# Two groups of heads share one PSUM bank in the weighing of an attention and mixture-of-experts block

## The reference

```python
# attention: 16 heads of 8; q and k are normalised 6-component line products
q = lines(bg @ W1_q.T, bg @ W2_q.T)        # bg = [x, x of the token before]
k = lines(x @ W1_k.T, x @ W2_k.T)
logits = einsum('bhtc,bhsc->bhts', q, k @ J6.T) * 6**-0.5
attn = softmax(where(causal, logits, -inf))
o = einsum('bhts,bhsd->bhtd', attn, (x @ Wv.T + bv) by heads)
x = layernorm(x + o @ Wo.T + bo)
# experts: a shared one, and the best 2 of 8 weighted by sigmoid(x @ Wr.T + rb)
x = layernorm(x + shared(x) + sum_of_two(weight * expert(x)))   # silu(x Wg) * (x Wu) Wd
```

## Time and profile before

| | us |
|---|---|
| median of 3 runs (lowest, highest) | 990.3 (988.67, 993.97) |
| span of the profiled execution, first to last instruction | 846.3 |
| between that span and the median of the runs | 144.0 |
| TensorE busy in the span | 713.0 |
| VectorE | 652.2 |
| GpSimd | 605.9 |
| ScalarE | 585.3 |

### The profile page before, as it was taken

How to read it: one execution, slowest core, us unless ns; L and a number is a source line. 1 busy time by engine, 2 the same in 40 slices (tenths; PEclk the granted TensorE clock), 3 DMA queues, 4 the chain that set the end, 5 groups by cost and what they waited for, 6 DMA issues and landing times.

```text
span 846.3 us, 23791 instructions
## 1 busy us (share of the span) xinstructions
PE 713.0 (84%) x7568; PEld 455.1 (54%) x7568; DVE 652.2 (77%) x1712; ACT 585.3 (69%) x907; POOL 605.9 (72%) x901
## 2 busy tenths in 40 slices
PE   2689998899998998899999988886899999999700
PEld 2334554454544554445545543475788888887600
DVE  7647798988789889788798794689667666665795
ACT  1478897688786886687887887553466666665456
POOL 4436666689887987698898887653177777777585
PEclk8689999899999999899999998899999999999955
DMA  7000111111111111101201102622663333331496
GB/s 255 14 14 13 38 39 38 52 56 47 51 59 41 50 56 36 58 28 53 68 31 50 45 32 85 210 89 77 170 189 96 100 109 103 102 98 53 121 277 200
DMA packets 88797, 69.89 MB, mean 83 GB/s; under 512 B 8292, under 2 KB 77158, under 8 KB 88720
## 3 DMA queue, kind: packets, MB, share of 16 engines
q1 hardware_dynamic: 69456, 43.43, 17.8%
q0 software_dynamic: 8512, 17.06, 6.1%
q10 hardware_dynamic: 10752, 8.39, 3.3%
HBM read 38.16 MB, written 31.21 MB: 82 GB/s over the span
## 4 chain that ended last, share of the span: by engine, by line
PE 54%; DVE 25%; issue 9%; ACT 6%; POOL 5%; DMA 1%; DVEq 0%; ACTq 0%; POOLq 0%
PE S L905 14%; PE O L727 12%; PE O L927 8%; PE S L712 7%; PE W L686 4%; ACT probs L1071 3%; PE W L752 3%; POOL probs L540 2%; DVE prodA L1276 2%; PE W L662 2%; PE W L943 2%; POOL prodB L528 1%; DVE stats L1686 1%; DVE hid L1634 1%; DVE hid L1613 1%
## 5 line engine op out<-in xcount | busy, mean ns | idle before, releaser
L1071 ACT ACTIVATE probs<-S 128x1024 f32<-128x1024 f32 x320 | 322.7, 1044 | 95.5 <-PE S L712 70.3
L540 POOL TENSOR_SCALAR_AFFINE_SELECT probs<-probs 128x256 f32<-128x256 f32 (+1 forms) x448 | 228.8, 541 | 101.1 <-ACT probs L1071 100.5
L619 POOL DMA_INDIRECT z_scratch<-y,rows x136 | 139.2, 1023 | 63.5 <-issue 36.9
L727 PE MATMUL O<-probs,v_aug 128*32 128x512 f32 (+3 forms) x2048 | 172.9, 458 | 11.9 <-POOL probs L540 11.9
L263 POOL DMA_INDIRECT rows_scratch<-xrow,slot_i x128 | 131.7, 1029 | 44.6 <-issue 27.8
L712 PE MATMUL S<-qkT 32*128 32x512 f16 (+3 forms) x1024 | 137.6, 311 | 17.6 <-ACT probs L1071 9.7
L1634 DVE TENSOR_TENSOR hid<-hid 128x512 f16<-128x512 f32 x100 | 69.3, 693 | 72.4 <-ACT hid L1203 72.4
L1184 ACT ACTIVATE silu<-S 128x512 f32<-128x512 f32 x100 | 59.7, 597 | 91.3 <-PE S L905 90.7
L905 PE MATMUL S<-xT_rt,w_T 128*128 128x256 f16 (+1 forms) x864 | 103.5, 267 | 2.3 <-DVE xT_rt L1595 1.7
L927 PE MATMUL O<-w_T,hid 128*128 (+1 forms) x1200 | 91.5, 221 | 15.1 <-DVE hid L1634 11.7
L712 PEld LDWEIGHTS S<-qkT 32*128 32x128 f16 x1024 | 39.1, 92 | 112.1 <-issue 40.6
(11 more groups left out here) (158 smaller groups left out, 1131.7 us busy)
## 6 DMA issues: line engine op xcount, KB each, us to landing
rows<-rows_scratch SPq DMA_DIRECT2D x64, 130.0 KB
z<-z_scratch SPq DMA_DIRECT2D x32, 256.0 KB, 4.1
xT<-in_x_cols ACTq DMA_DIRECT2D x16, 256.0 KB, 2.8
x_in<-in_L_attn_x ACTq DMA_DIRECT2D x16, 256.0 KB, 3.1
x_scratch<-x SPq DMA_DIRECT2D x16, 256.0 KB, 2.6
x1T_scratch<-x1T SPq DMA_DIRECT2D x16, 256.0 KB, 2.2
xT_sh<-x1T_scratch SPq DMA_DIRECT2D x16, 256.0 KB, 4.4
x_in<-x_scratch SPq DMA_DIRECT2D x16, 256.0 KB, 5.0
```

Of the source, the lines that this page charges most:

```text
L540: pool.affine_select(out=v, in_=v, compare_op=ALU.is_ge, fill=0.0, base=0, pattern=[[0, v.shape[1]], [1, P]], channel_multiplier=-1).then_ ...
L619: pool.indirect_dma_start(out=z_dram, in_=y[:, q, a, :], in_offset=None, out_offset=bass.IndirectOffsetOnAxis(ap=rows[:, q, a, P + 1:P + 2 ...
L727: mm = pe.matmul(O[g % 2][32 * j:32 * j + 32, kb * P:T], v_aug[:, par, kb, 4 * g + j, :], probs[:, g % 2, c, col:col + T - kb * P], start= ...
L1071: act.activation(probs[:, g % 2, c, :], S[(g + c) % 2][:, :], ACT.Exp, scale=-SCALE / SPLIT_UP ** 2).then_inc(s_exp, 1)
```

## The change

Groups 0 and 1 now write the same output bank `O[0]`, groups 2 and 3 `O[1]`. In `v_aug` the heads j of groups 2p and 2p+1 lie in one slot of 82 columns. The weight tile for an even group has values and ones in columns 0 to 8 as before; that for an odd group has them in columns 9 to 17, with zeros on both sides. The odd group accumulates onto the even one: only its first product starts the bank, only the last one of the odd group ends it. So a strip of 32 partitions holds two heads, in 18 rows.

`copy_out` runs once for each pair, for groups 0 and 1 where group 1 was copied, for 2 and 3 where group 3 was. `transpose_out` runs in two halves, with two token blocks each: four transposes into `W1` after `logits(1, 0)`, four into `W0` after `logits(1, 1)`. `normalise` has a reciprocal of 128x32 and a product of 128x256 for each half. Counts of the semaphores follow. The columns of Wv and bv, and the rows of Wo, are permuted on the host to the new order of heads. Not shown below: the same replacement of counts in `transpose_o`, `down_early`, the last batch's part, and the count of VectorE's steps.

```diff
+PAIRS = 2
+SLOT = DH + 1
+VW = 32 + SLOT
...
         xres = sb("xres", [P, 2, NT, P])
-        oT_raw = sb("oT_raw", [P, HP, T])
+        oT_raw = sb("oT_raw", [P, PAIRS, T])
         rden = sb("rden", [P, NT, H])
...
         qkT = sb_a("qkT", [P, 2, HP, 2, T], FP16)
-        v_aug = sb_a("v_aug", [P, 2, NT, H, 32])
+        v_aug = sb_a("v_aug", [P, 2, NT, H // 2, 2 * VW])
         probs = sb_a("probs", [P, 2, NCHUNK, CHUNK])
...
                         bounds_check=TAIL - 1, oob_is_err=False).then_inc(rows_out[par], 16)
+        def value_slots(par):
+            return v_aug[:, par].rearrange("p t n (g w) -> p (t n) g w", g=2)
+        def value_weights(par, kb, g, j):
+            return v_aug[:, par, kb, 4 * (g // 2) + j, 32 * (g % 2):32 * (g % 2) + 32]
...
             for par in range(2):
-                pool.memset(v_aug[:, par, :, :, DH:DH + 1].rearrange("p t h o -> p (t h) o"), 1.0)\
+                pool.memset(value_slots(par)[:, :, :, DH:DH + 1], 1.0)\
                     .then_inc(consts, 1)
...
-                pe.wait_ge(o_read, HP * b + g - 1)
+                if not (isinstance(b, int) and b == 0):
+                    pe.wait_ge(o_read, PAIRS * b + g // 2 - 1)
                 for _ in range(times):
-                    pe.matmul(O[g % 2][:, :], ident16[:, :], qkT[:, par, g, 0, :], start=True, stop=True)
+                    pe.matmul(O[g // 2][:, :], ident16[:, :], qkT[:, par, g, 0, :], start=True, stop=True)
...
                     pe.wait_ge(masked, NMASK * (n + 1))
-                    if not (isinstance(n, int) and n < 2):
-                        pe.wait_ge(o_read, n - 1)
+                    if g % 2 == 0 and not (isinstance(b, int) and b == 0):
+                        pe.wait_ge(o_read, PAIRS * b + g // 2 - 1)
                 for kb in blocks:
...
                         c, col = PIECES[(j, kb)]
-                        mm = pe.matmul(O[g % 2][32 * j:32 * j + 32, kb * P:T], v_aug[:, par, kb, 4 * g + j, :],
-                                       probs[:, g % 2, c, col:col + T - kb * P], start=(kb == 0), stop=(kb == NT - 1),
-                                       skip_group_check=True)
+                        mm = pe.matmul(O[g // 2][32 * j:32 * j + 32, kb * P:T], value_weights(par, kb, g, j),
+                                       probs[:, g % 2, c, col:col + T - kb * P], start=(g % 2 == 0 and kb == 0),
+                                       stop=(g % 2 == 1 and kb == NT - 1), skip_group_check=True)
                 if blocks[-1] == NT - 1:
...
-            def transpose_out(c, t, after):
-                if t == 0:
-                    pe.wait_ge(o_read, HP * (c + 1))
+            def transpose_out(c, half, after):
+                if half == 0:
+                    pe.wait_ge(o_read, PAIRS * (c + 1))
...
                         pe.wait_ge(rank_read, c)
-                elif t == 1:
-                    if after:
-                        pe.wait_ge(val_read, c + 3)
-                    else:
-                        pe.wait_ge(featT_read, HP * NB)
-                        pe.wait_ge(y_read, c)
-                elif t > 1:
-                    pe.wait_ge(outT_read, NT * c + t - 1)
-                for g in range(HP):
-                    mm = pe.transpose(W[(t + 1) % 2][:, g * P:(g + 1) * P], oT_raw[:, g, t * P:(t + 1) * P], ident[:, :])
+                elif after:
+                    pe.wait_ge(val_read, c + 3)
+                else:
+                    pe.wait_ge(featT_read, HP * NB)
+                    pe.wait_ge(y_read, c)
+                for a in range(2):
+                    t = 2 * half + a
+                    for pr in range(PAIRS):
+                        mm = pe.transpose(W[(half + 1) % 2][:, (PAIRS * a + pr) * P:(PAIRS * a + pr + 1) * P],
+                                          oT_raw[:, pr, t * P:(t + 1) * P], ident[:, :])
                 mm.then_inc(outT_full, 1)
...
             def transpose_o(c):
-                pe.wait_ge(outT_read, NT * (c + 1))
+                pe.wait_ge(outT_read, 2 * (c + 1))
                 for t in range(NT):
...
                 if not last:
-                    pe.wait_ge(outT_read, NT * (c + 1) + 3)
+                    pe.wait_ge(outT_read, 2 * (c + 1) + 1)
                 halves = xrow[:, par, :, 0, 0:P].bitcast(FP16)
...
                     transpose_out(b - 1, 0, not last)
-                    transpose_out(b - 1, 1, not last)
                 logits(1, 1)
                 if not first:
-                    transpose_out(b - 1, 2, not last)
-                    transpose_out(b - 1, 3, not last)
+                    transpose_out(b - 1, 1, not last)
                 logits(1, 2)
...
-                act.copy(v_aug[:, par, :, :, 0:DH].rearrange("p t h d -> p (t h) d"),
-                         W0[:, :].rearrange("p (n d) -> p n d", d=DH)).then_inc(val_read, 1)
+                act.copy(value_slots(par)[:, :, :, 0:DH],
+                         W0[:, :].rearrange("p (n g d) -> p n g d", g=2, d=DH)).then_inc(val_read, 1)
...
-            def copy_out(b, g):
-                act.wait_ge(pv_done, HP * b + g + 1)
-                if g == 0:
-                    act.wait_ge(outT_full, NT * b)
-                act.copy(oT_raw[:, g, :], O[g % 2][:, :]).then_inc(o_read, 1)
+            def copy_out(b, pr):
+                act.wait_ge(pv_done, HP * b + 2 * pr + 2)
+                if pr == 0:
+                    act.wait_ge(outT_full, 2 * b)
+                act.copy(oT_raw[:, pr, :], O[pr][:, :]).then_inc(o_read, 1)
...
                 if not first:
-                    copy_out(b - 1, 3)
+                    copy_out(b - 1, 1)
                 exps(b, 0, (4,))
...
                     copy_values(b + 1, 1 - par)
-                exps(b, 1, (0, 1, 2, 3))
-                copy_out(b, 0)
-                exps(b, 1, (4,))
+                exps(b, 1, range(NCHUNK))
                 if not first:
...
                     copy_rows(b - 2, par)
-                copy_out(b, 1)
+                copy_out(b, 0)
                 raise_weights(b, 1)
...
                 raise_weights(b, 2)
-                copy_out(b, 2)
                 exps(b, 3, (4,))
...
-            def normalise(c, t):
-                dve.wait_ge(outT_full, NT * c + t + 1)
-                w = W[(t + 1) % 2][:, :].rearrange("p (h n) -> p h n", n=32)
-                chain(dve.reciprocal(rden[:, t, :].rearrange("p (h o) -> p h o", o=1), w[:, :, DH:DH + 1]))
-                dve.tensor_tensor(o_tok[:, t, :].rearrange("p (h d) -> p h d", d=DH), w[:, :, 0:DH],
-                                  spread(rden[:, t, :].rearrange("p (h o) -> p h o", o=1), 2, DH), ALU.mult)\
-                    .then_inc(outT_read, 1)
+            def normalise(c, half):
+                dve.wait_ge(outT_full, 2 * c + half + 1)
+                w = W[(half + 1) % 2][:, :].rearrange("p (n k) -> p n k", k=32)[:, :, 0:2 * SLOT]
+                w = w.rearrange("p n (g d) -> p n g d", g=2)
+                r = rden[:, 2 * half:2 * half + 2, :].rearrange("p t (n g o) -> p (t n) g o", g=2, o=1)
+                chain(dve.reciprocal(r, w[:, :, :, DH:DH + 1]))
+                dve.tensor_tensor(o_tok[:, 2 * half:2 * half + 2, :].rearrange("p t (n g d) -> p (t n) g d", g=2, d=DH),
+                                  w[:, :, :, 0:DH], spread(r, 3, DH), ALU.mult).then_inc(outT_read, 1)
...
                     normalise(b - 1, 0)
-                    normalise(b - 1, 1)
                 if not last:
...
                 if not first:
-                    normalise(b - 1, 2)
-                    normalise(b - 1, 3)
+                    normalise(b - 1, 1)
                 if not last:
...
         parts += [q[:, 0:P].T, k.T.reshape(P, H, 4)[:, :, ::-1].reshape(P, H * 4)]
-    parts += [Wv.T, W1_q[:, P:2 * P].T, W2_q[:, P:2 * P].T, Wo.T, Wr.T, bv.reshape(P, 1)]
+    v = np.arange(P).reshape(2, 2, 4, DH).transpose(0, 2, 1, 3).reshape(P)
+    parts += [Wv.T[:, v], W1_q[:, P:2 * P].T, W2_q[:, P:2 * P].T, Wo.T[v], Wr.T, bv[v].reshape(P, 1)]
     return np.concatenate(parts, axis=1)
```

More of the change, by code:

```diff
@@ L983, in down_early @@
                 if m < 2:
-                    pe.wait_ge(o_read, HP * NB - 1 + m)
+                    pe.wait_ge(o_read, PAIRS * NB - 1 + m)
                 else:
@@ L1020, in _ @@
             gate_up_early(1)
-            for t in range(NT):
-                transpose_out(NB - 1, t, False)
-            pe.wait_ge(outT_read, NT * NB - 1)
+            for half in range(2):
+                transpose_out(NB - 1, half, False)
+            pe.wait_ge(outT_read, 2 * NB - 1)
             ranks(NB - 2)
@@ L1206, in _ @@
             early(0)
-            copy_out(NB - 1, 3)
+            copy_out(NB - 1, 1)
             early(1)
@@ L1507, in lower_weights @@
                                              op1=ALU.subtract).then_inc(w_lo, 1)
-            per = 4 + (4 + 9 + 2) + 2 + 1 + 13 + 3
+            per = 2 + (4 + 9 + 2) + 2 + 1 + 13 + 3
             base[0] = count[0]
@@ L1637, in _ @@
             early(0)
```

(4 more changed lines are left out.)

## The result

The changed kernel takes 981.67 us (median of 12 executions, 978.62 to 988.60) where the kernel before, on the same chip, takes 994.59 (984.96 to 1002.41): a ratio of 0.9907, 95% interval 0.9881 to 0.9934. Carried to the 990.3 us of the forecast the ratio makes 981.1, against 987.4 forecast.

A forecast was written before the change was run, and what follows sets the result against it. No engine saturated: the attention batch is a ring of hand-overs where TensorE's waits decide. Savings of 11.5 us less 8.6 us of clock falls gave -2.9 us: 990.3 to 987.4 us, range 977 to 1000.

The forecast's parts named there:

- the likeliest case: Whole kernel: -11.5 us of savings, 8.6 us paid back by clock falls, 987.4 us; chance 0.42.
- rival B: Attention stage: the clock holds, all but nothing is paid back, the gain of 11.5 us comes through, 978.8 us; chance 0.28.
- Transposes, 0 in mask bodies: Nine bodies where TensorE waits for GpSimd's masks after the transposes: gain 0, waits 0.65 become about 1.7, 1.52 become 2.6.
- the step on normalising: Merged reciprocals and products take 0.7 us off VectorE's chain, counted in five bodies with late features: 3.5 us off.
- The clock takes it back: TensorE behind lengthened mask waits: falls to 1.2 GHz cost 1.7 us (long) or 1.4 (short) each, 8.6 us taken.
- Rival C: All eight lengthened mask waits drop the clock, half for two stretches: +7.4 us, 997.7 us; chance 0.22.
- Bodies 1 and 2: 2.2 us: Attention batches without such waits: eight fewer transposes show fully on TensorE, 2 x 1.1 = 2.2 us off.
- Bodies with a late `next_slot`: 1.0 each: Four bodies where transposes stand right behind TensorE's long wait for VectorE: 1.0 us each, 4.0 us off.
- Evictions: 0.2 us in nine bodies: Two ScalarE copies fewer per batch; only group 0's, ahead of an exponential, counts: 1.8 us off in all.
- Start, +1.0: Kernel start: clearing the larger value tile takes 4.45 us instead of 3.47, on the path: 1.0 us added.
- 144 us around the span: Whole kernel: the profiled span is 846.3 us, the runs' median 990.3; the 144.0 us between were left unchanged.
- The meetings (D), 0.08: VectorE's `line_terms` products beside GpSimd's: one meeting more or less moves about 4 us; alone 986 or 994; chance 0.08.

The follow-up runs named there:

- the other two comparisons: The unedited changed kernel against the kernel before, repeated on two further chips: 985.29 us, ratio 0.9957, and 852.59 us, ratio 0.9976.
- the third trace: Profile of the unedited changed kernel from its repeat on the third chip, beside the kernel before: 852.59 us, ratio 0.9976.
- the two traces of the table: Two profiles of the unedited changed kernel, set body by body beside two of the kernel before; its timed runs there: 981.67 us (0.9907) and 852.59 us (0.9976).
- second profile of before: The kernel before, unedited, profiled once more: one execution of 866.28 us with a span of 864.5 us.

## Why the prediction was right, and where it was not

The forecast of a small gain, smaller than the work removed, holds. Its size is in part luck. 981.1 lies outside the likeliest case's own range (983 to 993) and nearer to the 979 of rival B, yet B's mechanism, a clock that holds, is not what the traces show; the other two comparisons (986.0, 987.9) lie at the likeliest case. And the terms below are off in both directions, while two executions of before lie 18 us apart and the forecast only 2.9 from no change. Step by step:

- **Transposes, 0 in mask bodies, the wait grows by what they took.** Right and shown: eight transposes put back leave a body at 30.8 us. The long waits are 2.5 (forecast 2.6). The short ones are 2.25, not 1.7; the missing 0.6 is in the step on normalising, which brings TensorE to the next `weigh` sooner: 1.5 with the normalising split, 2.25 with it merged. I had priced the two edits as if each ended in a different wait, but in a ring what one wait gives up, the next one takes.
- **The clock takes it back.** Right in kind and nearly in size. Behind a 2.5 us wait a fall makes 32.2 of 30.6: 1.6 forecast as 1.7. Behind a 2.25 us wait it makes 33.4 of 31.2 or 30.8: 2.2 to 2.6, forecast 1.4. In the third trace six of eight mask waits in bodies 5 to 12 have a fall, all four long ones and two of the four short, which is what I had assumed. But the split normalising shows 2.5 us waits with no fall behind them and falls behind 0.97, so the rule of before, that waits above 1.52 are at risk, is not the whole of it. (Rival C has a slip: seven falls of one stretch cost at most 3 x 1.7 + 4 x 1.4 = 10.7 by its own prices, so it takes all eight to outweigh the 11.5.) What the Trainium skill says (TensorE: Matmul & The Clock Gate, HAM oscillation) holds in kind: the clock swings between its two levels in a stream that waits interrupt. Its example has waits for DMA of about 3 to 5 us, and the trace shows the same swing behind waits of 2.3 to 2.5.
- **Bodies 1 and 2: 2.2 us.** 2.1 and 1.5 off in the two traces of the table.
- **Bodies with a late `next_slot`: 1.0 each.** Mixed: in bodies 3 and 4, which have it in every execution, 0 or worse (68.4 or 69.5 us before for both, 69.6 and 70.7 after); in later ones 34.3 to 34.8 for 33.7 to 38.2.
- **VectorE's chain: 0.7 us in five bodies.** The feature wait vanished, as said, but 0.4 of it shows. The product took 424 ns (forecast 419), the reciprocal 358, not 272: from 16 to 32 elements it grew by 106 ns, 6.6 ns an element, where I had used the product's 1.0. Busy, it is 1.56 us a batch for 1.38 forecast.
- **Evictions: 0.2 us in nine bodies.** 0.1 to 0.2 measured.
- **End, 1.0 off.** From the start of the last batch's transposes to those of `o_tok` it was 3.64 us (545.70 to 549.34) and is 2.78 in the third trace: 0.9.
- **Start, +1.0.** The clearing took 4.43 us (forecast 4.45) and GpSimd waited 8.33 (before 7.30), but the first feature transposes start at 24.63 and 24.55 us in two traces of the changed kernel and at 23.61 and 24.67 in the two of before: 1.0 later or nothing, and the traces don't settle which.
- **144 us around the span.** Wrong, but it cancels: terms of the attention stage were added to the median of the timed runs.
- **The meetings (D), 0.08.** This was underweighted. I took the four long waits of one execution for a fixed feature and gave them a saving of 1.0 each. The second profile of before had seven, and one wait added to before gave 0.9922. Between two executions of before the stage moved by 14.8 us, more than by any part of the change, and of 0.9907, 0.9957 and 0.9976 I can't say how much is fewer meetings. Waits for `next_slot` above 2.5 us from body 5 on number 2, 5, 2 and 5 in the four traces with 16 transposes and 2, 3, 2, 1, 3 and 3 in the six with 8 (products not in turn): it hints at fewer after the change, and doesn't show it.

So which part of the change makes the gain is not shown. The transposes have the best evidence, that they make none in the mask bodies. Without the merged normalising the ratio is 1.0062 (1.0009 to 1.0116) and with the evictions put back 1.0042 (0.9987 to 1.0098), which would give either of them all of the gain; but the changed kernel wasn't run on that chip, the two intervals overlap, and the bodies show only 0.4 and 0.1 to 0.2 us.

## What to carry to other kernels

Work taken away ahead of a wait for another engine only lengthens the wait, and if it is TensorE's it may cost the clock behind it: look at the granted clock after each wait that an edit will lengthen, and try harmless work in those. When two profiles of one kernel differ by more than the edit is worth, find what makes them differ first; here one added hand-over between two engines' products was worth as much as the whole change, and change, hand-over and filled wait together were worth 1.6%. Compare only runs from one chip.

## What the runs showed of the hardware that was not expected

**Chips differ.** The same kernel takes 994.59 and 994.25 us in two comparisons and 859.32 and 858.52 in two others. Most of the difference is in the expert stage, which the change doesn't touch: in two traces of the changed kernel, with spans of 982.2 and 848.8 us, some 123 of the 133 us come after 560 and 550 us. The window from 620 to 760 us, then the waits of ScalarE's first expert operation in it, for the changed kernel on the slower chip and on the faster one:

```profile
620.00:760.00 140.00, 104.48 (x1023) 86.27 (x1021) 60.47 (x114) 54.81 (x130) 56.46 (x58) 0.87 0.33 91
...
ACT silu L1192 <- remote: 45.7, 10, 4.8
...
ACT silu L1192 <- PE S L916: 30.4, 13, 4.7
```

```profile
620.00:760.00 140.00, 137.20 (x1622) 119.60 (x1622) 94.49 (x175) 93.49 (x226) 108.62 (x104) 1.00 0.39 105
...
ACT silu L1192 <- PE S L916: 47.1, 59, 1.5
```

In the same time the slower chip issues 1023 matmuls, the faster 1622. On the slower one ten waits of up to 4.8 us are put down to `remote`, another core or a queue that the profile doesn't know. Waits of TensorE before some scores, with nothing late that the trace names, are there too: 1.38 us at 439.91 in body 12, whose clock held and which still took 32.1. Of those over 1 us the five profiles with spans near 985 us have 0 to 10 in the attention stage, those with spans near 850 none. The cause of either kind wasn't tried and is open.

**Two engines' products.** Six products of VectorE beside six of GpSimd take 6.91 us in place of 1.40, while GpSimd's own longest product is 805 ns against a median of 512 in the second profile of before (1160 against 516 in the third of the changed kernel). The Trainium skill (SBUF — State Buffer, SBUF: two separate sides) tells of a port pair that a GpSimd instruction that reads SBUF and a VectorE one with two SBUF inputs can only hold in turn. The traces agree that they slow each other, and show most of it on VectorE.
